# Moving the two normalising scalings of the first stage from VectorE to ScalarE

## The reference, cut to what matters

```python
x = x + _L0_conv_ref(_gn(x), ...)   # 4-bit activations, 3x3 sign weights, batch norm, relu
x = x + _L1_conv_ref(_gn(x), ...)   # rfft2, amplitude and phase, a deformable 3x3
                                    # convolution of each, irfft2, abs, 5x5 convolution
```

## Time and profile before

| | |
|---|---|
| median of three runs | 7599.73 us |
| span of the profiled execution, from its first instruction to its last | 7593.5 us |
| time of that execution beyond its span | not given by the profile |
| TensorE matmul, busy | 5859.6 us, 77% |
| VectorE, busy | 4572.4 us, 60% |
| ScalarE, busy | 2753.9 us, 36% |
| GpSimd, busy | 5492.1 us, 72% |
| mean granted clock of TensorE | 0.875 |
| DMA moved | 540.78 MB, 71 GB/s |

### The profile page before, as it was taken

How to read it: one execution, slowest core, us unless ns; L and a number is a source line. 1 busy time by engine, 2 the same in 40 slices (tenths; PEclk the granted TensorE clock), 3 DMA queues, 4 the chain that set the end, 5 groups by cost and what they waited for, 6 DMA issues and landing times.

```text
span 7593.5 us, 104067 instructions
## 1 busy us (share of the span) xinstructions
PE 5859.6 (77%) x33682; PEld 2811.5 (37%) x33682; DVE 4572.4 (60%) x7421; ACT 2753.9 (36%) x5357; POOL 5492.1 (72%) x5044
## 2 busy tenths in 40 slices
PE   3578787788788788888888887887888878867666
PEld 2333333334333333344334443333333433332323
DVE  3366566566666766656665666667666566755541
ACT  2333333334333343434433343333434344332322
POOL 0177777777777777777777777777777777777760
PEclk7788898899888889988888998988999888988777
DMA  2222232222322323222332223223232233312120
GB/s 88 63 71 60 57 81 72 65 82 67 84 69 70 86 68 95 64 68 76 78 81 64 83 67 84 69 68 88 65 98 64 61 82 78 81 50 66 49 65 22
DMA packets 424825, 540.78 MB, mean 71 GB/s; under 512 B 310746, under 2 KB 318974, under 8 KB 417646
## 3 DMA queue, kind: packets, MB, share of 16 engines
q0 software_dynamic: 161280, 330.62, 16.6%
q1 hardware_dynamic: 262980, 203.17, 10.4%
HBM read 404.04 MB, written 116.94 MB: 69 GB/s over the span
## 4 chain that ended last, share of the span: by engine, by line
POOL 32%; PE 31%; issue 16%; DVE 14%; ACT 5%; DMA 1%; DVEq 1%; SPq 0%; POOLq 0%; ACTq 0%
POOL gath L584 32%; PE pair L1002 10%; PE ring L940 4%; PE ring L859 3%; PE ps_def L1023 2%; ACT u L1034 2%; PE ps_acc L976 2%; DVE prod L1578 2%; DVE gath L1596 2%; ACT prod L1234 1%; DVE gath L1602 1%; PE ring L904 1%; PE ring L805 1%; PE ring L915 1%; PE ring L821 1%
## 5 line engine op out<-in xcount | busy, mean ns | idle before, releaser
L584 POOL DMA_INDIRECT gath<-table_d,idx_all x5040 | 5491.9, 1090 | 1872.7 <-issue 1871.5
L1002 PE MATMUL pair<-clamp_x,tab 128*128 128x392 f32 (+1 forms) x5760 | 2793.7, 588 | 922.7 <-DVE prod L1578 895.9
L1578 DVE SCALAR_TENSOR_TENSOR prod<-prod,pair 128x392 f32<-128x392 f32 (+1 forms) x2880 | 1629.2, 569 | 1861.0 <-PE pair L1002 1806.5
L1234 ACT ACTIVATE prod<-ps_y,y_bias 128x392 f32<-128x392 f32 (+1 forms) x2880 | 1480.9, 597 | 2250.6 <-PE ps_acc L976 2199.6
L1002 PEld LDWEIGHTS pair<-clamp_x,tab 128*128 128x128 f32 x5760 | 1044.4, 210 | 2292.1 <-DVE prod L1578 1561.1
L1596 DVE TENSOR_TENSOR gath<-gath,wgt 128x1152 f32<-128x1152 f32 x560 | 756.9, 1352 | 368.6 <-DMA gath<-table_d,idx_all 367.9
L1034 ACT ACTIVATE u<-ring 128x448 f32<-128x448 f32 (+7 forms) x1376 | 603.4, 480 | 948.5 <-PE ring L904 244.5
L976 PE MATMUL ps_acc<-prod,w_samp 128*32 128x392 f32 (+1 forms) x5760 | 649.4, 523 | 6.5 <-DVE prod L1578 6.5
L1023 PE MATMUL ps_def<-xt,w_samp 32*32 32x224 f32 x5760 | 392.8, 438 | 140.3 <-DVE xt L1611 140.3
L1554 DVE TENSOR_SCALAR clamp_x<-ps_x 128x392 f32<-128x392 f32 (+1 forms) x720 | 410.4, 570 | 103.0 <-PE ps_x L959 103.0
L940 PE MATMUL ring<-u,w 128*32 128x392 f32 x5120 | 452.7, 511 | 23.5 <-ACT u L1034 23.5
(11 more groups left out here) (155 smaller groups left out, 4109.1 us busy)
## 6 DMA issues: line engine op xcount, KB each, us to landing
gath<-table_d,idx_all POOLq DMA_INDIRECT x5040
table_d<-u SPq DMA_DIRECT2D x192, 210.0 KB
point_d<-u SPq DMA_DIRECT2D x32, 406.0 KB
u<-point_d SPq DMA_DIRECT2D x32, 406.0 KB
u<-in_x SPq DMA_DIRECT2D x8, 1568.0 KB, 7.4
x_d<-u SPq DMA_DIRECT2D x8, 1568.0 KB, 6.8
xg_d<-u SPq DMA_DIRECT2D x8, 1568.0 KB, 5.6
u<-xg_d SPq DMA_DIRECT2D x32, 392.0 KB
```

The lines of the kernel that those rows point to most:

```text
L584: pool.indirect_dma_start(gath[:, k % BUFS, n * CELL:(n + 1) * CELL], None, table_d[:, :], bass.IndirectOffsetOnAxis(idx_all[:, k, n:n + 1 ...
L1002: nc.tensor.matmul(bank[:, 0:size], tab[:, b * NB + br, j * 128:(j + 1) * 128], clamp_x[:, s % 2, 0:size], start=True, stop=True)\
L1234: nc.scalar.activation(prod[:, s % 2, j, 0:size], ps_y[:, 0:size], ACT.Relu, bias=y_bias[:, j:j + 1]).then_inc(relu_ready, 1)
L1578: v.scalar_tensor_tensor(rows, rows, 1.0, bank[:, 0:size], ALU.min, ALU.mult)\
```

## The change

Both scalings become one activation each on ScalarE (`Identity`, with the factor as its scale and the offset as its bias). ScalarE waits on `chain_l0`, the count of VectorE's finished small steps, for factor and offset. After the first scaling it raises the new `scaled_ready`, on which VectorE waits ahead of the clip. After the second it raises `xg_ready` itself. The pieces at which they stand are the same as before: piece 5 of step 0 and piece 4 of step 1. VectorE's chain has two links fewer in a quad (19 in place of 21).

```diff
-DVE_L0, DVE_FFT, DVE_IDX, DVE_BACK = 21, 13, 11, 10
+DVE_L0, DVE_FFT, DVE_IDX, DVE_BACK = 19, 13, 11, 10
+L0_SCALES = (9, 19)
...
+        scaled_ready = sem("scaled_ready")
...
                         nc.scalar.activation(small[:, 6:7], small[:, 5:6], ACT.Sqrt).then_inc(std_ready, 1)
-                        for _ in range(5):
+                        for _ in range(2):
+                            yield
+                        act.wait_ge(chain_l0, f * DVE_L0 + L0_SCALES[0])
+                        nc.scalar.activation(l_t, l_x, ACT.Identity, bias=small[:, 9:10], scale=small[:, 8:9])\
+                            .then_inc(scaled_ready, 1)
+                        for _ in range(3):
                             yield
...
                     nc.scalar.activation(small[:, 6:7], small[:, 5:6], ACT.Sqrt).then_inc(std_ready, 1)
+                    yield
+                    yield
+                    act.wait_ge(chain_l0, f * DVE_L0 + L0_SCALES[1])
+                    nc.scalar.activation(l_t, l_x, ACT.Identity, bias=small[:, 9:10], scale=small[:, 8:9])\
+                        .then_inc(xg_ready, 1)
...
-                        link(v.tensor_scalar(l_t, l_x, small[:, 8:9], small[:, 9:10], ALU.mult, ALU.add))
-                        yield
+                        yield
+                        dve.wait_ge(scaled_ready, f + 1)
                         link(v.tensor_scalar(l_t, l_t, 0.0, LEVELS, ALU.max, ALU.min))
...
                     link(v.tensor_scalar(small[:, 9:10], small[:, 10:11], small[:, 8:9], -1.0, ALU.mult, ALU.mult))
-                    yield
-                    link(v.tensor_scalar(l_t, l_x, small[:, 8:9], small[:, 9:10], ALU.mult, ALU.add))
                     link()
-                    dve.sem_inc(xg_ready, 1)
```

## The result

The changed kernel takes **7574.24 us** (median of 11 runs, 7565.44 to 7583.53) against 7600.01 (11 runs, 7589.84 to 7608.3) for the kernel before, run beside it: ratio 0.9967, 95% interval 0.9959 to 0.9976, or 25.8 us less (18 to 31). The forecast was 7583, range 7566 to 7599, and chance 0.5 for faster. One execution of the kernel with the doubled scaling, further down, took 19222 us at a granted clock of 0.424 and is left out of its median and ratio.

What follows compares the result with a forecast made beforehand. The prediction took GpSimd's 5040 back-to-back indirect gathers to bound the kernel. Savings of 10.1 and 6.9 us, 17.0 in all, took the profiled span from 7593.5 to 7576.5; as a median 7583 us, range 7566 to 7599.

Steps and rivals of the forecast that it cites:

- The bound: From 337.6 to 7364.1 us GpSimd issues 5040 gathers without a pause; other engines matter only where they delay or lengthen these.
- The two ends of a stop (0.13 and 0.82): A gather stopped by a long SBUF-to-SBUF VectorE instruction ends 0.13 or 0.82 us after it, by how far it had come.
- ScalarE's time: The 128x3136 scaling was to take 2.82 us on ScalarE, against 1.91 on VectorE, extrapolated from two activation sizes.
- Second scaling, 10.1: In seven woven quads a gather of 2.39 us returns to 0.94 beside the second scaling: 10.1 us back.
- First scaling, 6.9: Gathers at the first scaling and clip, now stopped by the clip alone, give 6.9 us back, bounds 4 to 9.
- The page's figure: The skill page has a locked-out gather blocked until VectorE's end and about 115 ns; by it the sum is 4 us better.
- Prologue, costed at nothing: Before the gathers, ScalarE's longer scalings add 1.9 us, costed at nothing because the image store waits for table fills anyway.
- the sign named for "no cover" (339.5): A first gather at 339.5 us, not 337.6, would show the prologue's 1.9 us are not hidden behind the table fills.
- New waits at nothing: ScalarE's wait for the small factors and VectorE's 0.98 us longer wait for the clip were both costed at nothing.
- Rival B: Slower: ScalarE's scalings hold up the units in the loop quads, using up the buffer reserve of 25.2 us; 7610 us, chance 0.06.
- Rival A: Real gain, but under 15.2 us: GpSimd falls back in step with VectorE, losing whole gather steps; 7591 us, chance 0.44.
- The sum of 17.0: Total saving over the execution: 10.1 us at the second scaling plus 6.9 at the first.

Runs made afterwards that it cites:

- doubled scaling: The kernel before, with the second scaling done twice on VectorE in all eight quads: 7602.93 us against 7600.95, ratio 0.9999.
- statistics added to before: The kernel before, with three unused statistics instructions on VectorE ahead of the second scaling in all eight quads: 7592.7 us, ratio 0.9989.
- second alone: The changed kernel with the first scaling back on VectorE, only the second on ScalarE: 7576.96 us, ratio 0.9975 to the kernel before.
- semaphore: The kernel before, with the new semaphore raised by VectorE after its first scaling and awaited ahead of the clip: 7606.83 us against 7617.07, ratio 0.9986.
- gap filled: The changed kernel with three statistics instructions on VectorE where the second scaling stood, in the woven quads: 7574.85 us against 7589.48 before, ratio 0.9981.

## Why the prediction was right, by its own steps

- **The bound: right.** GpSimd issues back to back from the first gather to the last, and its 0.6 us of waiting for VectorE are no more than the 1.2 of the earlier trace rows. The 28.3 us between first and last gather went in the length of gathers (29.3 less busy).
- **The two ends of a stop (0.13 and 0.82): right** for the long instructions with one input. The slots' multiplications, which the prediction never priced, have the 0.82 alone: no gather that they stretch ends 0.13 after them.
- **ScalarE's time: mis-sized, by little.** 3.00 us in place of 2.82; the line through two shapes of 112 partitions missed 0.18, 6%. The clip starts 3.04 after the scaling's start, not 2.86.
- **Second scaling, 10.1: right**, to the last digit of the stretch, in both executions of the changed kernel.
- **First scaling, 6.9: right in size (6.6 and 8.1, counted with its clip), the phase wrong.** The prediction took quad 4's phase for five quads, because they repeated it before. They did not repeat it after: in the changed kernel's first execution the gather under the clip takes 2.38, 2.02, 2.56, 2.56, 2.06 and 1.94 in the six loop quads, and in the second only one of six takes 2.55. In quad 4, 2.56 stands where 2.45 was worked out, for the clip begins 0.18 later against ScalarE's start. Losses of 1.0 to 1.6 where 1.51 was forecast fall inside the stated bounds; that they add up to nearly the forecast is in part luck.
- **The page's figure.** The prediction set "SBUF — State Buffer" of the Trainium skill (section "A bandwidth-pool intuition that's wrong (but worth ruling out)") against the rows: blocked until VectorE's end and about 115 ns. The late-caught gathers agree (0.12 to 0.13), those caught at their start end 0.82 after, and quad 4's clip is one of them. The extra 4 us of saving by that figure did not show in the stretch: at the first place 8.8 and 7.2 are left.
- **Prologue, costed at nothing: not confirmed.** In the six executions with both scalings of quad 0 on VectorE the store was issued at 62.65 to 64.10 and landed at 97.90 to 100.76. In the four with both on ScalarE it was issued at 64.71 to 65.51 and landed at 98.49, 100.02, 101.06 and 104.52. On the mean that is 1.6 later out and 1.6 later in, as without any cover, but within spreads of 2.9 and 6.0. The first gather starts at 336.55 to 338.92 in the six, and at 336.80, 339.75, 341.54 and 347.57 in the four, so the sign named for "no cover" (339.5) appeared in three. Against it, the doubled scaling, issued at 65.61, landed at 98.52, and the statistics added to before, issued at 64.63, at 104.28. Whether the 1.9 us are covered stays open; they are small beside the 25.8.
- **New waits at nothing: right.** Waiting for the clip's input is 21.6 us of VectorE in seven quads, and no gap between gathers came of it. Rival B (7610) is out. The page that it drew on, "Perfetto Trace Analysis" ("Optimizing Scalar/DVE Operations") of the Trainium skill, was right on the durations, 3.00 against 1.91, and ScalarE in place of VectorE won all the same, since not VectorE's time but what it stops was the price.
- **Rival A** (gains of less than 15.2 us through phase) did not come true: the phases were redrawn, as it said, but no loss came of it. The sum of 17.0 was met by the direct terms (17.4 at the two scalings and the clip). What carried the result from 7583 to 7574 is about 8 us that no term of the prediction stands for and whose cause the runs leave open. It fell on the good side, which the range had left to chance: that part is luck.

## What to carry to other kernels

Where GpSimd's indirect DMAs bound a kernel, price a VectorE instruction by the gathers that it stops, not by its duration, and by its phase to them if it has two inputs in SBUF. Move or merge the long SBUF-to-SBUF ones, even to an engine that takes half as long again. Removed stops returned their own stretch within 12 us either way in ten of eleven kernels here, with 14 missing in the last, for reasons that are only in part known; so compare with a neutral edit of the kernel before as well as with the kernel before. And stop when the freed places are few beside the rest: here all 36.6 us at these places were removed in one kernel, while 297 stayed at the slots' first multiplications, and the time won (22.4 us) was no more than the change's.

## What the runs showed that I had not expected

- A multiplication of two SBUF operands (L1596, 1.35 us) stretches the gather that begins under it: 249 to 297 us a run, the largest item of all stretch. The addition that follows it in each slot (L1602, 128x576) comes next, with 172 to 177 us in every profile.
- Undisturbed gathers are 1.2500 us apart in some builds (before, second alone, semaphore, statistics, doubled, gap filled) and 1.2525 in the others. In the latter, ScalarE's 2304 ramps of 392 elements also take 1164.7 to 1164.9 us in all, where they take 1162.9 to 1163.2 in the former. The same in each execution of a kernel. Unexplained.
- ScalarE's three-microsecond activations from SBUF stopped no gather in any profile: nearly all gathers under them are undisturbed, and each stretched one ends 0.13 or 0.82 after a VectorE instruction.
- Chips differ: the same kernel before had medians of 7589.48, 7595.93, 7600.95 and 7617.07 us on four chips, a wider spread than the change is worth.
